# A graph-network layer pair: the first pass's state made during the preparation, and the set-up blocks of the pass loops run only from the second pass on

## The reference

```python
h = jnp.maximum(_layernorm(x, axis=-1), 0.0)
# layer 0: graph convolution
H = h @ W.T + b
H = (H - mean(H, 0)) * rsqrt(var(H, 0) + 1e-5) * gamma + beta
dinv = rsqrt(1.0 + segment_sum(ones, dst))
out = segment_sum(H[src] * (dinv[src] * dinv[dst])[:, None], dst) + H * (dinv * dinv)[:, None]
x = x + relu(out)
# layer 1: a three-layer perceptron over node, summed edge features and a global vector
h = jnp.maximum(_layernorm(x, axis=-1), 0.0)
agg = segment_sum(edge_attr, dst)
m = concatenate([h, agg, u[0] for every node], axis=1)
x = x + relu(relu(m @ W1 + b1) @ W2 + b2) @ W3 + b3
```

## Time and profile before

| | us |
|---|---|
| median of 3 runs (lowest to highest) | 1194.56 (1193.79 to 1196.52) |
| the profiled execution's own time | 1195.33 |
| its span, first to last instruction | 1193.6 |
| PE busy | 1013.2 (85%) |
| DVE busy | 586.6 (49%) |
| POOL busy | 585.2 (49%) |
| ACT busy | 499.0 (42%) |
| mean granted TensorE clock | 0.909 |

### The profile page before, as it was taken

How to read it: one execution, slowest core, us unless ns; L and a number is a source line. 1 busy time by engine, 2 the same in 40 slices (tenths; PEclk the granted TensorE clock), 3 DMA queues, 4 the chain that set the end, 5 groups by cost and what they waited for, 6 DMA issues and landing times. The chain is left out here.

```text
span 1193.6 us, 23689 instructions
## 1 busy us (share of the span) xinstructions
PE 1013.2 (85%) x9255; PEld 682.4 (57%) x9255; DVE 586.6 (49%) x1338; ACT 499.0 (42%) x894; POOL 585.2 (49%) x574
## 2 busy tenths in 40 slices
PE   3875599889888898888898988888988889999888
PEld 2654266556555565555565765555655556557645
DVE  7988264435443444444443644343544344443375
ACT  3255264334443334333444534343443344443376
POOL 4124604665555565556564165556555556550324
PEclk9787689999988998988998998899989999889889
DMA  6004433545454444444454445454535444451403
GB/s 163 3 2 139 148 130 119 168 131 166 123 165 127 143 152 151 137 150 144 127 166 123 137 129 166 126 160 139 163 123 163 131 136 157 123 165 55 121 1 108
DMA packets 87064, 154.65 MB, mean 130 GB/s; under 512 B 10966, under 2 KB 36884, under 8 KB 87004
## 3 DMA queue, kind: packets, MB, share of 16 engines
q1 hardware_dynamic: 71004, 121.11, 31.4%
q0 software_dynamic: 16000, 32.80, 9.8%
HBM read 147.46 MB, written 6.41 MB: 129 GB/s over the span
## 5 line engine op out<-in xcount | busy, mean ns | idle before, releaser
L968 POOL DMA_INDIRECT gathered<-scaled_h_table,index x500 | 519.1, 1038 | 456.9 <-PE ps_sums L1203 299.7
L980 ACT CAST counts_sb<-ps_counts 128x588 f16<-128x588 f32 x560 | 383.2, 690 | 591.7 <-PE ps_counts L1159 441.5
L1165 PE MATMUL ps_product<-counts_sb,table_sb 128*128 128x240 f16 x2744 | 474.8, 279 | 18.2 <-issue 17.8
L1159 PE MATMUL ps_counts<-key_hot,lo_hot 128*128 128x294 bf16 x1120 | 349.6, 317 | 64.4 <-ACT counts_sb L980 34.0
L1165 PEld LDWEIGHTS ps_product<-counts_sb,table_sb 128*128 128x128 f16 x2744 | 277.3, 102 | 83.5 <-issue 27.7
L1189 PE MATMUL ps_sums<-attr,attr_hot 128*32 128x128 f32 x2240 | 193.0, 287 | 44.4 <-issue 37.6
L1100 DVE TENSOR_TENSOR acc<-acc,ps_product 128x96 f32 (+1 forms) x137 | 37.4, 273 | 390.2 <-remote 216.8
L1042 DVE TENSOR_TENSOR key_hot<-key,iota_key 128x1176 bf16<-128x1176 f16 x280 | 214.0, 764 | 0.0
L1159 PEld LDWEIGHTS ps_counts<-key_hot,lo_hot 128*128 128x128 bf16 x1120 | 114.5, 104 | 145.3 <-ACT counts_sb L980 57.5
L1189 PEld LDWEIGHTS ps_sums<-attr,attr_hot 128*32 128x32 f32 x2240 | 111.1, 111 | 109.8 <-issue 108.5
L1037 DVE TENSOR_TENSOR lo_hot<-src_lo,iota_key 128x512 bf16<-128x512 f16 x280 | 119.0, 425 | 76.8 <-PE ps_counts L1159 75.0
(11 more groups left out here) (228 smaller groups left out, 713.7 us busy)
## 6 DMA issues: line engine op xcount, KB each, us to landing
attr<-in_edge_attr_dram SPq DMA_DIRECT2D x80, 1280.0 KB
gathered<-scaled_h_table,index POOLq DMA_INDIRECT x500
acc<-in_x_dram SPq DMA_DIRECT2D x4, 768.0 KB, 8.8
scaled_h_table<-table_sb SPq DMA_DIRECT2D x12, 256.0 KB, 2.3
xs<-in_x_dram SPq DMA_DIRECT2D x12, 256.0 KB, 5.2
out_dram<-y_ring SPq DMA_DIRECT2D x12, 256.0 KB, 2.3
attr<-in_edge_attr_dram SPq DMA_DIRECT2D x2, 320.0 KB
attr<-in_edge_attr_dram SPq DMA_DIRECT2D x1, 640.0 KB
```

What stands on the lines that cost most here:

```text
L968: pool.indirect_dma_start(gathered[:, n % GATHERS, g, :], None, table, bass.IndirectOffsetOnAxis(ap=index[:, s * CG + g, t:t + 1], axis=0) ...
L980: act.copy(counts_sb[s % 2][:, :, 2 * k * WT:(2 * k + 2) * WT] .rearrange("p h (t n) -> p t h n", n=WT), ps_counts[n % 2][:, :, 0:KEYS].re ...
L1159: pe.matmul(ps_counts[pair % 2][:, c, 0:KEYS], lo_hot[:, b, part, :, c], key_hot[:, b, part, :, c], start=True, stop=True).then_inc(built, 1)
L1165: ins = pe.matmul(ps_product[side][:, 0:SLOTS], table_sb[:, h, low, :], counts_sb[side][:, h, :], start=(part == 0), stop=(part == 2 * NB ...
```

## The change

Five edits belong together.

1. The preparation makes the arrays for the first window directly: `iota_w` starts at 0, `drow` (and by it `drel`), `slot_node` and `dense_node` lose the one step by which they were behind, so four fused operations with a constant become plain subtractions.
2. Two functions are new, `find_keys` and `begin_pass`. DVE calls both in the preparation block, between `bn_aggr` and the sum `dinv`. `find_keys` uses an array of its own, `within`, where `key_hot` had served.
3. The outer set-up block stands in a condition on the pass number: it runs from the second pass on. It clears the semaphores too.
4. The inner set-up block stands in a condition on the chunk pass number in the same way. Three of the semaphores are cleared by PE where ACT cleared them.
5. The wait for `table_out` moves from SP, at the end of the table block, to POOL, ahead of its first gather in the main block.

```diff
+        def find_keys(v, link):
+            link(v.tensor_scalar(within[:], flat(drel), 0.0, None, ALU.is_ge))
+            v.tensor_tensor(key[:], flat(drel), src_hi[:], ALU.add)
+            link(v.scalar_tensor_tensor(out=within[:], in0=flat(drel), scalar=float(WT), in1=within[:],
+                                        op0=ALU.is_lt, op1=ALU.mult))
+            v.tensor_tensor(key[:], key[:], within[:], ALU.mult)
+
+        def begin_pass(v, link):
+            v.tensor_copy(slot_now[:], slot_node[:])
+            v.tensor_copy(dense_now[:], dense_node[:])
+            link(v.tensor_copy(starts[:], chunk_start[:]))
+            v.tensor_scalar(starts_int[:], starts[:], float(N), None, ALU.min)
...
                     for k, r in enumerate(BLOCKS):
-                        v.scalar_tensor_tensor(out=drow[:, k, :].rearrange("g (t e) -> g t e", t=GT),
-                                               in0=edge_f[:, r, :].rearrange("g (t e) -> g t e", t=GT),
-                                               scalar=float(WT),
-                                               in1=tile_min[:, r, :].unsqueeze(2).to_broadcast([GB, GT, P]),
-                                               op0=ALU.add, op1=ALU.subtract).then_inc(tiles_ok, 1)
+                        v.tensor_tensor(drow[:, k, :].rearrange("g (t e) -> g t e", t=GT),
+                                        edge_f[:, r, :].rearrange("g (t e) -> g t e", t=GT),
+                                        tile_min[:, r, :].unsqueeze(2).to_broadcast([GB, GT, P]), ALU.subtract)\
+                         .then_inc(tiles_ok, 1)
...
                     v.bn_aggr(bn[:, 0:2], bstats[:].rearrange("p c k -> p (c k)")).then_inc(bn_ok, 1)
+                    v.wait_ge(turn_read, TURNS)
+                    find_keys(v, link)
+                    begin_pass(v, link)
                     v.wait_ge(placed_deg, R)
                     v.tensor_tensor(dinv[:], dinv[:], ps_x[:, 0:NB], ALU.add)
...
-                    sp.wait_ge(table_out, 16 * CHUNKS)
...
-            with nc.Fori(0, passes):
-                with nc.Block() as block:
-                    @block.vector
-                    def _(v):
-                        v.sem_clear(pass_step)
-                        link = chained(v, pass_step)
...
-                with nc.Fori(0, chunk_passes):
+            with nc.Fori(0, passes) as slot_pass:
+                with nc.If(slot_pass > 0):
                     with nc.Block() as block:
...
+                            find_keys(v, link)
+                            begin_pass(v, link)
+                with nc.Fori(0, chunk_passes) as chunk_pass:
+                    with nc.If(chunk_pass > 0):
+                        with nc.Block() as block:
...
                         @block.gpsimd
                         def _(pool):
+                            pool.wait_ge(table_out, 16 * CHUNKS)
                             for s in range(GN):
```

More of the change, by code:

```diff
@@ L92, in gnn_kernel @@
         key = sb("key", [P, DN * CT], F16)
+        within = sb("within", [P, DN * CT], F16)
         index = sb("index", [P, GB, GT], I32)
@@ L714, in gnn_kernel @@
         table_sb = sb("table_sb", [P, NB, 2, P], F16)
+        table_out = sem("table_out", ctx)
         ROWS = 3
@@ L937, in _ @@
                             link = chained(v, pass_step)
-                            v.tensor_scalar(slot_now[:], slot_now[:], -float(WC), None, ALU.add)
-                            v.tensor_scalar(dense_now[:], dense_now[:], -float(WC), None, ALU.add)
-                            link(v.tensor_scalar(starts[:], starts[:], float(WC), None, ALU.add))
-                            v.tensor_scalar(starts_int[:], starts[:], float(N), None, ALU.min)
+                            v.tensor_scalar(iota_w[:], iota_w[:], float(W), None, ALU.add)
@@ new lines, in _ @@
+                            v.tensor_scalar(slot_node[:], slot_node[:], float(W), None, ALU.add)
+                            v.tensor_scalar(dense_node[:], dense_node[:], float(WT), None, ALU.add)
+                            link(v.tensor_scalar(flat(drel), flat(drel), -float(WT), None, ALU.add))
+                            find_keys(v, link)
[3 more added lines that the diff above has]
+                        with nc.Block() as block:
+                            @block.sync
+                            def _(sp):
+                                for s in (summed, rows_used, last_in, *attr_in):
+                                    sp.sem_clear(s)
+                            @block.tensor
+                            def _(pe):
+                                for s in (hots, built, saved):
+                                    pe.sem_clear(s)
+                            @block.scalar
+                            def _(act):
+                                for s in (multiplied, product_saved, product_turned, product_ready):
+                                    act.sem_clear(s)
+                            @block.gpsimd
+                            def _(pool):
+                                pool.dma_reset()
+                                for s in (attr_hots, rows_hots, sums_saved, rows_saved, place_hots, placed, added, *gather_in):
+                                    pool.sem_clear(s)
+                            @block.vector
+                            def _(v):
+                                v.sem_clear(pass_step)
+                                link = chained(v, pass_step)
+                                v.tensor_scalar(slot_now[:], slot_now[:], -float(WC), None, ALU.add)
+                                v.tensor_scalar(dense_now[:], dense_now[:], -float(WC), None, ALU.add)
+                                link(v.tensor_scalar(starts[:], starts[:], float(WC), None, ALU.add))
+                                v.tensor_scalar(starts_int[:], starts[:], float(N), None, ALU.min)
```

37 lines of the change are left out of this document (12 added, 25 removed).

## The result

The changed kernel took 1187.11 us (median of 5, 1185.24 to 1194.59), the kernel before 1194.56 on the same chip (median of 5, 1193.53 to 1196.67). The ratio is 0.9952, with a 95% interval of 0.9931 to 0.9972. That is 5.7 us less by the ratio (3.3 to 8.2) and 7.45 less by the medians.

The account below looks back on a forecast made before the run. PE bounds the main block; before it, 106 to 115 us is a serial chain. Terms -6.9, +1.5 and +0.1 give -5.3 us: 1190.0 for the profiled execution, median 1189.3, own range 1187.8 to 1191.5, overall 1185.3 to 1194.3.

Parts of the forecast that it names:

- The sum: Whole kernel: -6.9 + 1.5 + 0.1 = -5.3 us, with bounds of -3.1 and -6.8.
- The main block's start, -6.9: Between table and main block: wait and set-ups go, 1.47 us remain; start at 108.3 instead of 115.19 us.
- The preparation, +1.5: End of preparation: 3.9 us of moved DVE work, 2.42 covered by waiting for PE; `dinv` 1.5 us late.
- The DMA overlap, +0.1: First edge-feature load shares DMA engines with the table's last writes: +0.1 us, at most 0.3.
- POOL's new wait, nothing: Ahead of POOL's first gather: the wait for the table's writes holds POOL up by next to nothing.
- The rival of the jumps: At the taken branches: a jump waits for an instruction fetch, 2.2 us, leaving -3.1 us; chance 0.13.
- The rivals of the first step: PE's pauses, 127 to 145 us: swallow the earlier start (near 1194, chance 0.10) or shrink (1184, chance 0.10).
- The slower rival: Main loop: PE's code lies further back and stops more often, +8.7 us, median 1198; chance 0.10.

Follow-up runs that it names:

- first pair: Profiled executions of the changed kernel and the kernel before from the first timing, no further edit; medians 1187.11 and 1194.56 us.
- the wait alone: Kernel before with only SP's wait for the table's writes moved to POOL: 1192.34 us, ratio 0.9983; on the even chip 982.41 us, ratio 0.9983.
- the repetition: The changed kernel measured once more, no edit, against the kernel before: 1188.48 us, ratio 0.996.
- the run that was to test it: Changed kernel with POOL's first gather held back until DVE has built three sets of hot rows: 979.27 us, ratio 0.9955.
- the state alone: Changed kernel with SP's wait for the table's writes put back in the table block: 1190.38 us, ratio 0.9956.
- no jumps: Changed kernel with the two conditional set-up blocks left out, so only for one-pass data: 1191.19 us, ratio 0.9971.
- the far jump: Changed kernel with 600 never-executed semaphore clears per engine inside the outer conditional block: 984.28 us, ratio 1.0004.

## Why the prediction was right, step by step

The sum was right and so were its largest terms: -5.3 forecast; -4.8 (-2.7 to -6.7) when measured again, -5.1 (-3.4 to -6.9) by the ratio on the even chip, and -5.95 in the traces of that chip at PE's first use of a load. The medians differ by more, 6.6 and 6.3 us. So the forecast was some 0.6 too small by the even chip's traces, and the 7.45 of the first medians, which lies beyond the sum's own bound of 6.8, holds a part of chance. That the total came so near owes something to luck, as the parts show.

- **The main block's start, -6.9.** It measured -6.99: 8.35 or 8.36 us between the last write's issue and the load became 1.36 or 1.37, on both chips, where 1.47 was forecast. The parts inside were split differently: I had 0.27 for the barrier, 0.8 for two entries and 0.4 for two branches. Without the branches and their tests 0.54 are left, so the barrier and the entries cost half of what I took, and the branches 0.82, twice of it. The two errors, 0.53 and 0.42 us, cancel, and that is luck; the whole term would else have been 0.4 to 0.5 us off. I had taken the entry as an upper bound from the earlier trace rows and used most of it, and 0.2 for a branch without a row.
- **The preparation, +1.5.** `dinv` is 1.26 us late in the first pair, 0.13 of it not by the change, and 0.94 on the even chip. `find_keys` and `begin_pass` take from 83.42 to 87.06, some 3.6 us where I counted 3.9. Counted from the start of POOL's memset, which is free of what came before, `dinv` is 1.12 us late in the first pair and 1.13 on the even chip: the term was 0.4 too large.
- **The DMA overlap, +0.1.** PE starts on the load 5.99 us after its issue, for 6.15; on the even chip 5.98 for 6.21. So it is 0.2 faster, not slower. That too is within the scatter: the kernel before with the wait alone moved shows 6.24 on one chip and 5.99 on the other. Only with an even earlier load is there a sign of a price, the 6.56 us without the jumps.
- **POOL's new wait, nothing.** It is the releaser of the first gather, and that gather comes 0.6 us after the load. Nothing is late by it.
- **The rival of the jumps** was wrong for this kernel and right as a mechanism. With 600 instructions to jump it takes 3.1 us on SP, more than the 2.2 that I took from the smallest write, and instruction packets move in that time. The median lost more than that, and the trace lays the rest to the clock and to the stretch behind the loop.
- **The rivals of the first step.** The pauses were not shortened in the first pair (5.95 and 5.14 us, for 5.30 and 3.68), and in the repetition they were 3.86 and 4.67: their sum scatters about the old one. The start was not swallowed: the lead at the first product was 7.35 us there and 7.14 on the even chip. Why the pauses exist on one chip and not on two others stays open; the run that was to test it fell on a chip without them.
- **The slower rival, stops that depend on the loop's place,** finds no support. 600 more instructions ahead of the loop left its steps at 28.15 us, but on a chip that has no stops in either kernel. The traces with stops settle more. With the loop in its old place PE's stops without a visible releaser before `ps_sums` are 56 and 62, with 37.6 and 41.9 us (before; the wait alone). In its new places they are 63, 59, 63 and 59, with 40.8, 44.2, 41.1 and 43.4 us (the changed kernel twice; the state alone; no jumps). All such stops of PE from 200 to 1100 us together are 66.0 and 62.7 us in the old place, 65.3 to 67.1 in the new. And from the first to the last product the loop takes 929.1 and 930.9 us in the old place, 927.7 to 935.6, with a mean of 930.4, in the new.

## What to carry to other kernels

A serial stretch between two blocks (wait for a write, barrier, set-up, barrier) is worth nearly its full length when no engine has other work there, and its set-up can be made earlier under a wait that another engine causes. The part that runs over that cover is paid in full, so look for what else lengthens the covered chain: here one small operation held up by POOL's memset was worth about 3 us in the traces, half as much as the whole change. A jump over a few instructions is cheap, 0.4 us with its test, but one over hundreds cost 3 us on SP and more on POOL.

## What the runs showed of the hardware

**The same kernel is 211 us shorter on two other chips.** The middle of the changed kernel's main block, first on the first chip:

```profile
200.00:1100.00 900.00, 796.50 (x7793) 529.80 (x7790) 399.28 (x873) 360.85 (x630) 482.64 (x468) 0.92 0.45 141
```

and on an even one:

```profile
200.00:850.00 650.00, 649.92 (x7182) 466.74 (x7180) 371.69 (x810) 338.49 (x580) 476.36 (x447) 1.00 0.57 185
```

PE is busy without a gap there, at a granted clock of 1.00, and each full step takes 28.15 us, where most take 35 to 38 on the first chip. The stops without a visible releaser are absent in both kernels. So they are no property of the kernel alone, and a gain is better measured where they are absent. What causes them was not found.

**An operation of DVE can end with a memset of POOL.** The f32 128x128 operation with one tensor input took 3.67 us beside the memset and ended within 0.1 us of it; with that operation gone, the f16 one with two inputs took 0.87 us in the midst of the memset. "SBUF — State Buffer" of the Trainium skill, section "🔬 SBUF: two separate sides", describes an exclusive lock on a pair of ports that DVE in a two-port mode and GpSimd share; these two rows agree with it.

**The stretch behind the loop is longer where the clock is low at its start.** The first of the eight-microsecond stretches of the perceptron, in the changed kernel and in the kernel before, both on the same even chip:

```profile
899.00:907.00 8.00, 7.93 (x41) 6.50 (x42) 2.16 (x6) 4.12 (x15) 3.50 (x4) 0.81 0.81 237
...
906.00:914.00 8.00, 6.79 (x28) 5.47 (x29) 0.69 (x1) 2.28 (x8) 2.67 (x3) 0.58 0.81 228
```

From the copy of the last product to the end the first takes 79.6 us and the second 82.7, so this pair overstates the gain by 3.1 us at the end. All 14 traces of this case fall in line, whatever the kernel and the chip. With a clock of 0.79 to 0.81 in the first eight us of the perceptron the stretch from the last product takes 79.6 to 80.1 us (four traces), with 0.64 to 0.69 it takes 80.9 to 81.1 (six), and with 0.50 to 0.58 it takes 82.7 to 83.7 (four, the far jump among them). The same changed kernel shows all three: 79.6, 80.9 and 82.7. So a difference of two or three us between two executions can come from here, and a gain in the loop or ahead of it is read at the last product. What makes the clock fall in one execution and not in the next was not found.
